# Split first loads, two banks for late outputs, and three moved operations in a six-stage decoder kernel

## The chip, the cores and the metric

The kernel runs on one core of one Trainium2 chip. The metric is device time in microseconds (us). The engines are TensorE (PE in the profile; its weight loads are PEld), VectorE (DVE), ScalarE (ACT), GpSimd (POOL) and SyncE (SP), whose queue issues most DMAs.

## The reference

Input `x` is 32 sequences ("items") of 100 rows by 256, and a context of 32 x 361 x 192. Six residual blocks follow one another, each on a plain layer norm of `x`:

```
x = x + self_attention(norm(x))              # 16 heads of 16, causal
x = x + cross_attention(ctx, norm(x), mask)  # 4 heads of 64, keys: ctx rows and latents
x = x + block(norm(x))                       # rope attention, then 8 experts, top 2
x = x + rotated_attention(norm(x))
x = x + wide_cross_attention(norm(x), ctx)   # 16 heads of 64
x = x + shared(norm(x)) + experts(norm(x))   # shared MLP 256-1024-256, and top 2 of 8 experts
```

In the last block every row is sent to two experts, and their outputs are weighted and added to the row, as is the output of the shared MLP.

## The kernel before

All 32 items stay in on-chip memory as `g.x`. There is one block of code for each stage: `self_phase`, `normed_cross_phase`, `mix_phase` (the "mixed" stage), `rotation_phase`, `wide_cross_phase` and `expert_phase`. Between two stages all engines meet. Within a stage the order of the work is written out by hand, for each engine apart, in pairs of items; semaphores tie the engines to one another, and each engine works strictly down its own list.

**Self stage.** SP issues the list `g.loads` in order, each load with the semaphore of its set. The set `first` holds 8 items, the qkv weights, the constants and the projection weights; `rest` holds the other 24 items. PE, ACT and DVE all begin with a wait for the whole of `first`. PE then runs `WARM` = 4 products on the qkv weights that nobody reads, and goes on to `make_rows` (L259, which transposes the normed pair), `make_q`, `make_k` (L266), `make_v` (L281), `mask` and `scores` (L296). DVE measures a pair (L85, L89), POOL takes the root (L94, L96), DVE applies it (L101), and ACT copies every bank out (L408 for the transposed rows).

**Cross stage.** SP loads the context rows (`load_cross_raw`) of a pair into one buffer, `raw`, as soon as the statistics of the pair before are taken (`cstats`). At the head DVE does `keep_kv` (L2093), measures the keys (L2103, L2107), and scales them with `norm_k` (L2112) once POOL has the root (L1688). `ctx_stats(SECOND)` (L2074 to L2085) stands between `norm_k(FIRST, 0, 1)` and `norm_k(FIRST, 1, 0)`. PE's `turn_k` (L1785) transposes the scaled keys.

**Mixed stage.** ACT's list begins with `apply(1)` (L1196, which norms the second pair and waits for POOL's offset at L768), then `keep_rows(0)` (L1133), then `keep_rope(0)` (L1137). PE transposes the normed first pair (L862), waits until it is copied, transposes the rope rows (L862 again) and makes q (L880).

**Expert stage, its end.** When the 57 tiles of the experts are done, POOL gathers the two expert rows of each item by two indirect DMAs (L3731), with a one-column add to `combine_hold` (L3729) ahead of them. DVE adds them to `g.x` (`combine`, L4074 and L4076) and copies the indices for the item 8 further on. Meanwhile PE does the shared MLP of the seven pairs 1, 3, ..., 13: hidden layer (L3539), turn of the next pair (L3549), output (`later_out`, L3834) into one bank, `out_bank`. `add_later` (L4087) adds that bank to `g.x`; `later_out(j)` waits for `add_later(j - 1)`, which stands behind `combine(4j + 1)` in DVE's list. SP stores the items in order (L3695), those of the seven pairs after their `add_later`.

## Time and profile before

| | |
|---|---|
| median of 3 runs | 3362.42 us (3358.3 to 3364.45) |
| profiled execution, device time | 3364.29 us |
| its span, first to last instruction | 3362.4 us |
| mean granted TensorE clock | 0.98 of full speed |
| PE busy | 3202.7 us (95%) |
| DVE, ACT, POOL busy | 53%, 48%, 44% |

All starts below are microseconds from the start of the span. A timeline row reads: start, length, engine, line, operation, output and inputs, how many instructions are merged; in brackets how long the engine stood idle before it, and who released it. The granted clock is a share of 2.4 GHz: 0.50 is 1.2 GHz.

### The profile page before, as it was taken

How to read it: one execution, taken by the hardware profiler on the slowest of the kernel's cores; microseconds unless marked ns; L12 is line 12 of the kernel's file. 1: busy time of each engine (PE TensorE's matmuls, PEld its weight loads, DVE VectorE, ACT ScalarE, POOL GpSimd, SP SyncE). 2: the span in 40 equal slices, each digit the busy share in tenths (PEclk: the TensorE clock that was granted, in tenths of full speed). 3: DMA queues.
4: the chain of work that ended last, by engine and by line, in shares of the span. 5: the costliest groups of instructions: out<-in, count | busy, mean ns of one | idle time of the engine just before them, and what ended most of it. 6: DMA issues, size and time to landing. Idle time of an engine off the chain costs nothing. (4 is left out here: it accounts for less than half of the span.)

```text
span 3362.4 us, 71194 instructions
## 1 busy us (share of the span) xinstructions
PE 3202.7 (95%) x26568; PEld 2352.6 (70%) x26569; DVE 1772.9 (53%) x5682; ACT 1607.3 (48%) x3295; POOL 1494.3 (44%) x1990
## 2 busy tenths in 40 slices
PE   7998999998999779998999999999999999999998
PEld 5775566666777644444676777767777688999997
DVE  4666777765888556543455544554445565111114
ACT  4654666665666047884555445545455511111111
POOL 1002444433676146651665656655666564000017
PEclk9999999998999889999999999999999999999999
DMA  8700111100001650000000000000000013999963
GB/s 244 290 2 14 43 43 44 43 15 14 17 23 29 172 143 24 21 16 26 14 8 8 8 8 15 8 8 8 8 14 1 2 40 118 325 327 323 325 237 104
DMA packets 111490, 263.34 MB, mean 78 GB/s; under 512 B 24003, under 2 KB 70240, under 8 KB 95840
## 3 DMA queue, kind: packets, MB, share of 16 engines
q1 hardware_dynamic: 90208, 224.70, 21.0%
q0 software_dynamic: 16384, 26.29, 2.8%
q10 hardware_dynamic: 4608, 8.39, 0.7%
q8 instruction: 194, 3.18, 0.4%
q14 instruction: 96, 0.79, 0.1%
HBM read 196.61 MB, written 62.65 MB: 77 GB/s over the span
## 5 line engine op out<-in xcount | busy, mean ns | idle before, releaser
L3004 POOL TENSOR_SCALAR wide_probs<-wide_probs,wide_inverse 100x361 f32<-100x361 f32 x504 | 594.5, 1192 | 0.1
L3297 ACT ACTIVATE wide_probs<-wide_probs,wide_least 100x361 f32<-100x361 f32 x512 | 301.0, 592 | 6.8 <-DVE wide_least L3410 6.8
L3410 DVE CUSTOM_DVE_ANT_0 wide_probs<-banks,wide_bias 100x361 f32<-100x361 f32 x512 | 251.5, 529 | 42.8 <-issue 37.7
L3056 PE MATMUL banks<-w_wide_v,wide_c 64*120 64x512 f32 (+1 forms) x1152 | 266.0, 591 | 0.0
L3050 PE MATMUL banks<-wide_c,w_wide_k 64*128 64x361 f32 x1536 | 257.1, 467 | 2.3 <-PEq L4101 2.3
L2588 ACT ACTIVATE rot_h<-banks,w_rot_b 128x800 f32<-128x800 f32 x256 | 223.3, 923 | 54.7 <-PE banks L2414 49.1
L3002 POOL TENSOR_TENSOR wide_hold_pool<-eps 100x1 f32<-100x1 f32 x252 | 48.6, 193 | 444.7 <-DVE wide_inverse L3416 444.7
L3891 ACT ACTIVATE tiles_hT<-banks 128x512 f32<-128x512 f32 x114 | 68.1, 597 | 349.1 <-PE banks L3807 349.1
L3807 PEld LDWEIGHTS banks<-tiles_xT,tiles_w 128*128 128x128 f32 x1824 | 214.7, 194 | 4.7 <-issue 1.8
L3807 PE MATMUL banks<-tiles_xT,tiles_w 128*128 128x128 f32 x1824 | 215.3, 277 | 1.2 <-DVE tiles_xT L4053 1.2
L3050 PEld LDWEIGHTS banks<-wide_c,w_wide_k 64*128 64x128 f32 x1536 | 150.5, 188 | 90.8 <-issue 4.6
L3083 PE MATMUL banks<-wide_kT,wide_qT 64*100 64x361 f32 x1024 | 207.4, 476 | 1.8 <-issue 0.7
L3820 PE MATMUL banks<-tiles_w,tiles_hT 128*128 128x256 f32 x912 | 206.4, 379 | 0.3 <-issue 0.3
L3729 POOL TENSOR_TENSOR combine_hold<-eps 100x1 f32<-100x1 f32 x32 | 7.9, 246 | 434.0 <-DMA slots<-tiles_out 433.2
L3056 PEld LDWEIGHTS banks<-w_wide_v,wide_c 64*120 64x120 f32 (+1 forms) x1152 | 120.7, 180 | 106.0 <-issue 93.9
L3820 PEld LDWEIGHTS banks<-tiles_w,tiles_hT 128*128 128x128 f32 x912 | 168.8, 190 | 21.0 <-issue 0.4
L3291 ACT COPY wide_v<-banks 120x512 f32<-120x512 f32 (+1 forms) x96 | 56.2, 585 | 222.5 <-PE banks L3056 222.5
L3101 PEld LDWEIGHTS banks<-ident,wide_probs 100*120 100x120 f32 (+1 forms) x1536 | 139.7, 138 | 30.1 <-issue 28.2
L3101 PE MATMUL banks<-ident,wide_probs 100*120 100x100 f32 (+1 forms) x1536 | 155.9, 251 | 0.8 <-ACT wide_probsT L3303 0.8
L3113 PE MATMUL banks<-wide_probsT,wide_v 120*64 120x100 f32 (+1 forms) x3072 | 147.8, 251 | 4.1 <-ACT wide_probsT L3303 4.0
L3288 ACT COPY wide_kT<-banks 128x361 f32<-128x361 f32 x128 | 59.0, 461 | 193.2 <-PE banks L3050 193.2
L3113 PEld LDWEIGHTS banks<-wide_probsT,wide_v 120*64 120x64 f32 (+1 forms) x3072 | 134.6, 136 | 20.6 <-issue 17.6
(499 smaller groups left out, 7173.2 us busy)
## 6 DMA issues: line engine op xcount, KB each, us to landing
tiles_w<-in_moe_w SPq DMA_DIRECT2D x114, 1024.0 KB, 5.2
slots<-zeros SPq DMA_DIRECT2D x58, 512.0 KB, 6.6
cross_c<-in_ctxT SPq DMA_DIRECT2D x32, 270.8 KB, 4.4
wide_c<-in_ctxT SPq DMA_DIRECT2D x32, 270.8 KB, 4.1
mix_kT<-slots SPq DMA_DIRECT2D x32, 256.0 KB, 4.3
slots<-mix_m_tiles_out ACTq DMA_DIRECT2D x32, 256.0 KB, 4.1
tiles_rows<-slots SPq DMA_DIRECT2D x57, 128.0 KB, 4.8
slots<-tiles_out SPq DMA_DIRECT2D x57, 128.0 KB, 5.0
```

The lines of the kernel that those rows point to most:

```text
L2588: nc.scalar.activation(t.h[:, u % 2, m, 2 * half:2 * half + 2, :], pair_banks(i), ACT.Tanh, bias=w.b1[:, m:m + 1]).then_inc(h_done[i], 1)
L3004: last = nc.gpsimd.tensor_scalar(t.probs[:, i, j, :], t.probs[:, i, j, :], t.inverse[:, i, j:j + 1], None, ALU.mult)
L3050: last = nc.tensor.matmul(make_bank(unit, lane)[:, 0:CTX], w.k[rows_of(lane), k, at:at + P], g.wide_c[rows_of(lane), of.buf, k, :], start= ...
L3056: last = nc.tensor.matmul(make_bank(unit, lane)[0:kw, :], g.wide_c[rows_of(lane), of.buf, k, k0:k0 + kw], w.v[rows_of(lane), k, of.hf * BA ...
L3083: last = nc.tensor.matmul(scores(j), t.qT[rows_of(j), here.hf, m, lane, :], t.kT[rows_of(j), here.hf, m, lane, :], start=True, stop=True)
L3101: last = nc.tensor.transpose(turned(bank)[0:cols, at], t.probs[:, i, j, k0:k0 + cols], g.ident[0:S, 0:S])
L3113: last = nc.tensor.matmul(out[rows_of(j), :], t.v[0:kw, of.hf, k, LANE_OF(i), at:at + WD], t.probsT[0:kw, group % STEP_GROUPS, bank, cols] ...
L3297: last = nc.scalar.activation(t.probs[:, i, j, :], t.probs[:, i, j, :], ACT.Exp, bias=t.least[:, i, j:j + 1], scale=-1.0, accum_out=t.rows ...
L3410: last = nc.vector.tensor_tensor_reduce(t.probs[:, i, j, :], scores(j), t.bias[:, :], -1.0, LARGEST, ALU.add, ALU.min, t.least[:, i, j:j + 1])
L3807: last = nc.tensor.matmul(out_, t.w1[:, lane, c, m * P:(m + 1) * P], t.xT[:, lane, c, :], start=(c == 0), stop=(c == DC - 1))
L3820: last = nc.tensor.matmul(tile_out, t.hT[:, lane, m, :], t.w2[:, lane, m, :], start=(m == 0), stop=(m == HM - 1))
L3891: nc.scalar.activation(t.hT[:, lane, half * HALF_HID:(half + 1) * HALF_HID, :].rearrange("p m r -> p (m r)"), hid_bank(lane, half), ACT.Si ...
```

## The change

- Self stage: the loads are cut into sets `pair` (2 items), `turn` (the identity), `qkv`, `first` (constants, items 2 to 7, projection weights), `near` (items 8 to 11 and two constants) and `rest`. Each step waits for the set that it reads. PE runs 3 unread products, on a buffer of zeros, before it waits for any load. ACT runs one exponential on a constant column, before its first wait on another engine's work.
- Cross stage: the context rows of the second pair are loaded by SP at the end of its self-stage list. `ctx_stats(SECOND)` and `ctx_root(SECOND)` stand ahead of the first pair's work.
- Mixed stage: ACT's `apply(1)` comes after `keep_rows(0)` and `keep_rope(0)`.
- Expert stage: `later_out` alternates between banks 6 and 7 and waits for the `add_later` two before; the add to `combine_hold` and its semaphore are gone; the last `add_later` stands after the last `combine`, and SP stores the last of the seven pairs at the end.

```diff
+NEAR_ITEMS = 12
+SELF_WARM = 3
...
             with sp.Fori(0, FILLS) as k:
...
+            sp.wait_ge(cs.cstats, 1)
+            for lane in range(LANES):
+                load_cross_raw(sp, near, lane, LANES + lane, ctx_in)
...
         def _(pe):
-            pe.wait_ge(g.loaded.first, g.total.first)
-            pe.wait_ge(s.ones, 1)
-            pe.wait_ge(s.parts_zero, 1)
-            for k in range(WARM):
-                nc.tensor.matmul(make_bank, w.qkv[:, 0, 0:P], w.qkv[:, 0, 0:BANK], start=True, stop=True)
+            pe.wait_ge(g.loaded.filled, 3)
+            for k in range(SELF_WARM):
+                nc.tensor.matmul(make_bank, g.zeros[:, 0:P], g.zeros[:, 0:BANK], start=True, stop=True)
+            pe.wait_ge(g.loaded.turn, g.total.turn)
...
             def make_q(p):
                 pe.wait_ge(s.yT, p + 1)
+                if p == 0:
+                    pe.wait_ge(g.loaded.qkv, g.total.qkv)
...
             def mask(b):
                 if b > 0:
                     pe.wait_ge(s.shifted, b)
+                else:
+                    pe.wait_ge(g.loaded.first, g.total.first)
...
         def _(act):
-            act.wait_ge(g.loaded.first, g.total.first)
-            act.wait_ge(s.picked, 1)
+            act.wait_ge(g.loaded.filled, 3)
+            nc.scalar.activation(t.begun[:, :], g.eps[:, :], ACT.Exp)
...
             def keep_k(p, edge):
+                if p == 0:
+                    act.wait_ge(s.picked, 1)
...
         def _(dve):
-            dve.wait_ge(g.loaded.first, g.total.first)
-            nc.vector.memset(parts_out, 0.0).then_inc(s.parts_zero, 1)
-            nc.vector.reduce_sum(t.own[:, :], g.own_scaled[:, :].rearrange("p (j i) -> p i j", i=EDGES), AX.X).then_inc(s.picked, 1)
-
             def stats(p):
-                if p == 2:
+                if p == 0:
+                    dve.wait_ge(g.loaded.pair, g.total.pair)
+                elif p == 1:
+                    dve.wait_ge(g.loaded.first, g.total.first)
+                elif p == 2:
+                    dve.wait_ge(g.loaded.near, g.total.near)
+                elif p * LANES == NEAR_ITEMS:
                     dve.wait_ge(g.loaded.rest, g.total.rest)
...
             stats(0)
+            nc.vector.memset(parts_out, 0.0).then_inc(s.parts_zero, 1)
             apply(0)
+            dve.wait_ge(g.loaded.first, g.total.first)
+            nc.vector.reduce_sum(t.own[:, :], g.own_scaled[:, :].rearrange("p (j i) -> p i j", i=EDGES), AX.X).then_inc(s.picked, 1)
...
+                if k + 1 == 0:
+                    apply(1)
                 if is_lane(n):
                     weigh(n)
...
-                if is_pair(k + MIX_AHEAD):
+                if k + MIX_AHEAD > 1 and is_pair(k + MIX_AHEAD):
                     apply(k + MIX_AHEAD)
...
-            for k in range(1, TURNS + 1):
+            for k in range(2, TURNS + 1):
...
             rows_root(SECOND)
+            ctx_root(SECOND)
             add_bias(FIRST)
...
             q_root(FIRST)
-            ctx_root(SECOND)
             add_bias(SECOND)
...
             rows_stats(SECOND)
+            ctx_stats(SECOND)
             dve.wait_ge(s.row, 1)
...
             norm_k(FIRST, 0, 1)
-            ctx_stats(SECOND)
             norm_k(FIRST, 1, 0)
...
+        later_bank = lambda j: g.psum[0:S, 6 + j % 2, :]
...
-            for b in range(B):
+            in_last_pair = lambda b: b // LANES == LATER_PAIRS[-1]
+            for b in sorted(range(B), key=in_last_pair):
                 sp.wait_ge(z.rows, b + 1)
...
                 pool.wait_ge(z.slots, b + 1)
-                nc.gpsimd.tensor_tensor(v.hold[:, k:k + 1], g.eps[0:S, :], g.eps[0:S, :], ALU.add).then_inc(z.held, 1)
...
             def later_out(j):
-                if j > 0:
-                    pe.wait_ge(z.shared, j)
+                if j > 1:
+                    pe.wait_ge(z.shared, j - 1)
...
                 if b + GATHER < B:
-                    dve.wait_ge(z.held, b + 1)
                     dve.wait_ge(z.rows, b + 1)
...
-                if step == 1 and j > 0:
+                if step == 1 and 0 < j < LATER:
                     add_later(j - 1)
+            add_later(LATER - 1)
...
+                load_items("pair", 0, LANES)
+                load_constant("turn", "ident")
+                self_w = Fields(qkv=weight(own, "qkv", "self_qkv", [P, DC, 3 * D]))
+                for n in ("own_scaled", "causal", "ident_b"):
+                    load_constant("first", n)
+                load_items("first", LANES, first_pairs)
                 self_w["proj"] = weight(own, "first", "self_proj", [P, DC, D])
+                load_items("near", first_pairs, NEAR_ITEMS)
+                for n in ("ones", "before"):
+                    load_constant("near", n)
+                load_items("rest", NEAR_ITEMS, B)
```

How the lists of the engines stand at three places follows. First VectorE at the head of the cross stage, from the second pair's row statistics on; before:

```order
L2063 TENSOR_SCALAR cross_rvareps<-cross_rmeanvar 100x2
L2093 SCALAR_TENSOR_TENSOR cross_kv<-banks,cross_crstd,cross_row 121x2x256 x2
...
L2112 TENSOR_TENSOR cross_kv<-cross_kv,cross_kroot 121x512
L2074 BN_STATS cross_cstats<-cross_raw 121x6 x6
L2077 MEMSET cross_hold 121x1
L2080 BN_AGGR cross_cmeanvar<-cross_cstats 121x2 x6
L2085 TENSOR_SCALAR cross_cvareps<-cross_cmeanvar 121x6
L2112 TENSOR_TENSOR cross_kv<-cross_kv,cross_kroot 121x512 x2
```

and in the changed kernel:

```order
L2083 TENSOR_SCALAR cross_rvareps<-cross_rmeanvar 100x2
L2094 BN_STATS cross_cstats<-cross_raw 121x6 x6
L2097 MEMSET cross_hold 121x1
L2100 BN_AGGR cross_cmeanvar<-cross_cstats 121x2 x6
L2105 TENSOR_SCALAR cross_cvareps<-cross_cmeanvar 121x6
L2113 SCALAR_TENSOR_TENSOR cross_kv<-banks,cross_crstd,cross_row 121x2x256 x2
...
L2132 TENSOR_TENSOR cross_kv<-cross_kv,cross_kroot 121x512 x3
```

The fourteen instructions of the context statistics stood between the second and the third key scaling; they now stand ahead of the first `keep_kv`, and the last three scalings follow each other.

Second ScalarE at the head of the mixed stage (`mix_y` is the normed pair, `mix_yT` and `mix_m_ropeT` the transposed rows); before:

```order
L1196 ACTIVATE mix_y<-x,mix_m_offset,mix_ln_rstd 100x256 x2
L1133 COPY mix_yT<-banks 128x400
L1137 COPY mix_m_ropeT<-banks 128x400
L1142 ACTIVATE mix_qT<-banks,w_mix_in_b 128x200
L1149 ACTIVATE mix_kT<-banks,mix_m_k_bias,mix_own 128x200 x2
```

and in the changed kernel:

```order
L1151 COPY mix_yT<-banks 128x400
L1155 COPY mix_m_ropeT<-banks 128x400
L1214 ACTIVATE mix_y<-x,mix_m_offset,mix_ln_rstd 100x256 x2
L1160 ACTIVATE mix_qT<-banks,w_mix_in_b 128x200
L1167 ACTIVATE mix_kT<-banks,mix_m_k_bias,mix_own 128x200 x2
```

Two copies have moved ahead of the two instructions that norm the second pair.

Third VectorE at the end of the program, the last items' `combine` (two rows each) and the last `add_later` (100x512); before:

```order
L4087 TENSOR_TENSOR x<-x,banks 100x512
L4074 SCALAR_TENSOR_TENSOR x<-combine_got,moe_gate,x 100x256
L4076 SCALAR_TENSOR_TENSOR x<-combine_got,moe_gate,x 100x256
L4074 SCALAR_TENSOR_TENSOR x<-combine_got,moe_gate,x 100x256
L4076 SCALAR_TENSOR_TENSOR x<-combine_got,moe_gate,x 100x256
```

and in the changed kernel:

```order
L4095 SCALAR_TENSOR_TENSOR x<-combine_got,moe_gate,x 100x256
L4097 SCALAR_TENSOR_TENSOR x<-combine_got,moe_gate,x 100x256
L4095 SCALAR_TENSOR_TENSOR x<-combine_got,moe_gate,x 100x256
L4097 SCALAR_TENSOR_TENSOR x<-combine_got,moe_gate,x 100x256
L4107 TENSOR_TENSOR x<-x,banks 100x512
```

The add of the last pair has moved behind the last two items.

## Rows read from the trace of the kernel before

**Rows 1.** The page, chain that ended last: share of the span by engine.
```profile
PE 18%; POOL 1%; DVE 0%; DMA 0%; issue 0%; SPq 0%; ACT 0%; DVEq 0%
```

**Rows 2.** Windows: stretch, length, busy PE, PEld, DVE, ACT, POOL, clock, DMA, GB/s.
```profile
50.00:150.00 100.00, 98.47 (x1109) 77.85 (x1108) 63.41 (x102) 60.76 (x92) 8.82 (x26) 1.00 0.93 342
```

**Rows 3.** Timeline of the first 22 us.
```profile
0.80 0.95 POOL L230 MEMSET zeros<- 128x1024 f32 x1
...
9.10 0.39 DVE L488 MEMSET banks<- 128x400 f32 x1 [8.98 <-DMA w_self_proj<-in_self_proj]
...
9.64 6.54 PE L250 MATMUL banks<-w_self_qkv 128*128 128x512 f32 x8 [9.64 <-DVE banks L488]
...
12.20 0.41 DVE L101 TENSOR_SCALAR self_y<-x,self_ln_meanvar,self_ln_rstd 100x256 f32<-100x256 f32 x1 [0.45 <-POOL self_ln_rstd L96]
...
16.02 0.51 PE L259 MATMUL banks<-ident,self_y 100*128 100x100 f32 x4
...
16.63 1.28 ACT L408 ACT_TABLE_LOAD   x1 [16.50 <-PE banks L259]
...
18.47 2.73 PE L266 MATMUL banks<-self_yT,w_self_qkv 128*128 128x200 f32 x8 [1.95 <-ACT self_yT L408]
```

**Rows 4.** Windows of the first loads; the last column is GB/s.
```profile
1.50:3.00 1.50, 0.00 (x0) 0.00 (x0) 0.00 (x0) 0.00 (x0) 0.52 (x2) 1.00 0.41 118
3.00:4.50 1.50, 0.00 (x0) 0.00 (x0) 0.00 (x0) 0.00 (x0) 0.00 (x0) 1.00 1.06 302
4.50:6.00 1.50, 0.00 (x0) 0.00 (x0) 0.00 (x0) 0.00 (x0) 0.00 (x0) 1.00 0.96 348
```

**Rows 5.** Timeline of the head of the cross stage.
```profile
306.80 1.41 DVE L2093 SCALAR_TENSOR_TENSOR cross_kv<-banks,cross_crstd,cross_row 121x512 f32<-121x512 f32 x2 [3.08 <-PE banks L1746]
...
319.76 3.23 POOL L1688 TENSOR_TENSOR cross_kroot<-cross_kclip,neg_half 121x8 f32<-121x8 f32 x2 [0.65 <-DVE cross_kclip L2107]
...
320.98 1.65 DVE L2074 BATCH_NORM_STATS2 cross_cstats<-cross_raw 121x6 f32<-121x192 f32 x6
...
323.37 1.28 DVE L2112 TENSOR_TENSOR cross_kv<-cross_kv,cross_kroot 121x512 f32<-121x512 f32 x2
...
324.20 3.33 PE L1785 MATMUL banks<-ident,cross_kv 124*128 124x124 f32 x16 [4.55 <-DVE cross_kv L2112]
```

**Rows 6.** Timeline of the head of the mixed stage.
```profile
769.97 0.51 PE L862 MATMUL banks<-ident,mix_y 100*128 100x100 f32 x4
...
771.31 0.78 POOL L785 TENSOR_TENSOR mix_m_rope<-mix_m_rope_a,mix_m_rope_b 100x256 f32<-100x256 f32 x1
...
774.44 1.09 ACT L1196 ACTIVATE mix_y<-x,mix_m_offset,mix_ln_rstd 100x256 f32<-100x256 f32 x2 [12.76 <-POOL mix_m_offset L768]
...
776.05 0.90 PE L862 MATMUL banks<-ident,mix_m_rope 100*128 100x100 f32 x4 [5.58 <-ACT mix_yT L1133]
```

**Rows 7.** Windows of two slow stretches, in the self and the cross stage.
```profile
19.00:29.00 10.00, 8.25 (x22) 6.29 (x21) 0.00 (x0) 1.57 (x3) 0.00 (x0) 0.50 0.93 190
...
322.00:332.00 10.00, 7.80 (x34) 5.86 (x36) 3.89 (x19) 1.85 (x2) 4.01 (x4) 0.53 0.21 57
```

**Rows 8.** Timeline of the end.
```profile
3264.88 1.02 POOL L3731 DMA_INDIRECT combine_got<-slots,combine_slot_i  x1 [0.30 <-issue]
...
3283.77 9.62 PE L3834 MATMUL banks<-w_moe_shared,combine_hidden 128*100 128x256 f32 x32 [4.67 <-DVE x L4087]
...
3298.98 7.07 PE L3834 MATMUL banks<-w_moe_shared,combine_hidden 128*100 128x256 f32 x32
...
3356.42 0.69 DVE L4087 TENSOR_TENSOR x<-x,banks 100x512 f32<-100x512 f32 x1 [4.25 <-PE banks L3834]
...
3358.45 0.48 DVE L4076 SCALAR_TENSOR_TENSOR x<-combine_got,moe_gate,x 100x256 f32<-100x256 f32 x1
```

**Rows 9.** The gathers' line: durations in ns, first and last start; time to landing.
```profile
L3731 POOL DMA_INDIRECT combine_got<-slots,combine_slot_i x64: 1007/1018/1290, 3263.5 to 3352.9; - x64
...
DMA to landing us min/median/max: 2.8/3.0/4.0
```

More of the change, by code:

```diff
@@ L175, in self_phase @@
         t = buffers(nc, ctx, "self", y=[S, TURNS, LANES, D], yT=[P, DC, LANES, S], qT=[P, TURNS, DC, LANES, S], kT=[P, TURNS, DC, EDGES, LANES, S], v=[S, TURNS, LANES, NH, HD + 1],
-                    rowmax=[S, 2, NH], probs=[S, 2, NH, S], probsT=[S, NH, S], parts=[P, ROUNDS, S], rowsum=[S, 2, NH], heads=[S, 2, D], headsT=[P, DC, S], own=[P, EDGES])
+                    rowmax=[S, 2, NH], probs=[S, 2, NH, S], probsT=[S, NH, S], parts=[P, ROUNDS, S], rowsum=[S, 2, NH], heads=[S, 2, D], headsT=[P, DC, S], own=[P, EDGES], begun=[P, 1])
         m1 = norm_of(nc, ctx, "self_ln")
@@ L3576, in expert_phase @@
         t = buffers(nc, ctx, "tiles", w1=[P, LANES, DC, HID], w2=[P, LANES, HM, D], rows=[P, LANES, D], xT=[P, LANES, DC, P], hT=[P, LANES, HM, P], out=[P, LANES, D])
[L3578 removed]
+        z = semaphores(nc, ctx, "combine", "slots half rows y yT_ready yT out_ready shared")
         later_hid_ready, later_hid = ([ctx.enter_context(nc.semaphore(f"combine_{n}{half}")) for half in range(2)] for n in ("hid_ready", "hid"))
         gathered, stored = ([ctx.enter_context(nc.semaphore(f"combine_{n}{k}")) for k in range(GATHER)] for n in ("gathered", "stored"))
[L3581 removed]
+        v = buffers(nc, ctx, "combine", got=[S, GATHER, 2, D], y=[S, LANES, D], yT=[P, DC, LANES, S], hidden=[P, HM, LANES, S])
         gather_i = ctx.enter_context(nc.sbuf_tensor("combine_slot_i", [S, GATHER, 2], I32))
@@ L3833, in later_out @@
                             pe.wait_ge(later_hid[m // HALF_HID], j + 1)
-                        last = nc.tensor.matmul(out_bank[:, lane * D:(lane + 1) * D], v.hidden[:, m, lane, :], w.shared2[:, m, :], start=(m == 0), stop=(m == HM - 1))
+                        last = nc.tensor.matmul(later_bank(j)[:, lane * D:(lane + 1) * D], v.hidden[:, m, lane, :], w.shared2[:, m, :], start=(m == 0), stop=(m == HM - 1))
                 last.then_inc(z.out_ready, 1)
@@ L4086, in add_later @@
                 rows = g.x[:, b:b + LANES, :].rearrange("s l d -> s (l d)")
-                nc.vector.tensor_tensor(rows, rows, out_bank, ALU.add).then_inc(z.shared, 1)
+                nc.vector.tensor_tensor(rows, rows, later_bank(j), ALU.add).then_inc(z.shared, 1)
             apply_later(1)
@@ L4113, in decoder @@
         g.psum = ctx.enter_context(nc.psum_tensor("banks", [P, 8, BANK], F32))
-        sets = "first rest cross mix mix_b rot wide moe cleared"
+        sets = "pair turn qkv near first rest cross mix mix_b rot wide moe cleared"
         g.loaded = Fields(**{n: ctx.enter_context(nc.semaphore("loaded_" + n)) for n in sets.split() + ["filled"]})
@@ L4168, in decoder, with load_items, load_constant @@
             with ExitStack() as own:
-                load("first", g.x[:, 0:first_pairs, :], i["x"][0:first_pairs].rearrange("b s d -> s b d"))
-                self_w = Fields(qkv=weight(own, "first", "self_qkv", [P, DC, 3 * D]))
-                for n in ("ident", "own_scaled", "causal", "ident_b", "ones", "before"):
-                    t = g[n]
-                    load("first", t[tuple(slice(None) for _ in t.shape)], i[n].bitcast(t.dtype))
+                def load_items(which, start, end):
+                    load(which, g.x[:, start:end, :], i["x"][start:end].rearrange("b s d -> s b d"))
+                def load_constant(which, n):
+                    load(which, g[n][tuple(slice(None) for _ in g[n].shape)], i[n].bitcast(g[n].dtype))
+                load_items("pair", 0, LANES)
[4 more added lines that the diff above has]
+                load_items("first", LANES, first_pairs)
                 self_w["proj"] = weight(own, "first", "self_proj", [P, DC, D])
-                load("rest", g.x[:, first_pairs:B, :], i["x"][first_pairs:B].rearrange("b s d -> s b d"))
+                load_items("near", first_pairs, NEAR_ITEMS)
+                for n in ("ones", "before"):
+                    load_constant("near", n)
+                load_items("rest", NEAR_ITEMS, B)
                 g.loads += cross_loads + mix_loads + rot_loads + moe_loads
```

5 lines of the change are left out of this document (3 added, 2 removed).

## The prediction

> **What bounds the kernel now.** I read the chain that ended last first [rows 1]: PE has by far the largest share, and what is not on it is small. Then the windows of the self loop [rows 2]: PE busy 98.47 of 100 us. So in the loops an earlier start passes through unchanged, and a gain can only come from stretches in which PE stands idle or runs at the lower of its two clocks. The timeline shows four of these, and the four parts of the change sit on them: PE's first useful work at 16.02 [rows 3]; 4.55 us idle at the head of the cross stage [rows 5]; 5.58 us idle at the head of the mixed stage [rows 6]; 4.67 us idle in the last hundred microseconds, followed by output products that take 9.62 instead of 7.07 us [rows 8]. I take the four as independent: each stage begins when all engines have met, and what follows waits for data of its own stage.
>
> **First loads.** Before, every engine waited for the last load of `first`; VectorE went on at 9.10, the normed pair was ready at 12.20 + 0.41 = 12.61, but PE was inside its unread products until 9.64 + 6.54 = 16.18, so the transposes ran at 16.02, and then ScalarE loaded its function table for 1.28 us before it could copy; q began at 18.47 [rows 3]. After: the pair is 205 KB. The queue had moved 1.5 x 118 = 177 KB by 3.0 us and goes on at 302 GB/s [rows 4], so the pair is in at about 3.1. The identity (66 KB) and qkv (786 KB) make 1057 KB, in at 4.5 + (1057 - 630)/348 = 5.7. VectorE needed 3.5 us from its wait to both normed items, 0.39 of it for the memset, which now lies in its wait for the root: 3.2 + 3.1 = 6.3. PE: the zeros are filled at 1.75; six product records at the length of before, 6.54/8 = 0.82 to 0.85 us each, from 1.9 to 7.0. So the transposes start at 7.0, not at 6.3: the unread products are what is late next. Without the table load the rest takes 0.51 + 0.1 + 0.49 + 0.05: q at 8.2 instead of 18.47, **-10.3 us**. The other loads are not met: `first` lands near 9 as before and is needed by the mask and the second copy of k, ten microseconds later; `near` is 443 KB more, near 10.5, and wanted after the first scores. If the pair lands 2 us late, transposes start at 8.3 and the term is -9.0.
>
> The clock belongs to this term. From 19 to 29 it was granted at 0.50, with PE busy 8.25 of 10 us [rows 7]; q took 2.73 us [rows 3]. In the self loop at 1.00 the same eight records take 1.6 us, by the ratio of the two levels (2.73/2 = 1.4, plus the weight loads) an estimate. q, k, v and their like at full clock are worth about 4.1 us. Before, the clock fell in the 1.95 us in which PE waited for the table and the copy. In the new order this gap is about 0.6 us, so if the unread products bring the clock up, it stays up. Whether 5.1 us of them are enough no row tells: nothing excludes either. I take half, **-2.0**, and keep 0 and -4.1 as ends.
> The Trainium skill ("TensorE: Matmul & The Clock Gate", What's actually happening) says that PE's recent activity sets the clock and that the point of the rise varies from run to run; the trace agrees as far as it shows a fall behind a gap, and by that page both ends are possible for one and the same kernel.
> The Trainium skill ("ScalarE: Activation LUTs", What ACT_TABLE_LOAD costs) gives 1.28 us for the load and a further 1.38 us of drain for a switch. This trace shows 1.28, and the copy 0.02 us behind it, so there is no drain here; with it the sum would be 1.4 us larger.
>
> **Cross stage.** The context statistics of the second pair took VectorE from 320.98 to 323.37 + 0.1, in front of the last two key scalings. Their roots came from POOL at about 321.4 and 323.0 (two operations, 3.23 us from 319.76), so the first scaling can start at 321.4 instead of 323.37 and PE's transposes at 322.25 instead of 324.20; the second scaling ends at 323.7, before PE has done the first half (half of 3.33 us): **-1.9 us** [rows 5]. In the new place the 2.45 us start at 303.7, where VectorE's wait of 3.08 us for the first keys began, and end at 306.2; that wait ended at 306.80 [rows 5]; margin 0.6. Without that cover (rows not loaded in time) it would cost up to 2.45. They are loaded some 35 us ahead, behind SP's last zero fill, and nothing but SP waits there. POOL's root for them, 1.3 us, moves to 306.2, where POOL had nothing urgent. The stretch after this gap ran at 0.53 [rows 7]; a gap that is 1.9 us shorter may keep the clock up, worth up to 2.5 us more. I take 0 for that and keep 2.5.
>
> **Mixed stage.** PE had transposed the first pair by 770.5, and the rope rows were ready at 771.31 + 0.78 = 772.1, but ScalarE stood in `apply(1)` until 774.44 + 1.09 and copied only then [rows 6]. Now it copies at 770.6 to 771.1; PE's second transposes start at 772.2 instead of 776.05: **-3.85 us**. `apply(1)` then begins at 774.44 as before, when its offset is there, and ends at 775.5; it is wanted by nothing before the second pair, and the copy of q, at 772.2 + 4.6 = 776.8, comes after it. If it did collide it would cost 1.1 us. Lower end -2.7, upper end -3.85 - 4, if the clock stays up there too.
>
> **The end.** (a) With two banks the second output follows its hidden layer: 4.67 us of idle and 9.62 - 7.07 = 2.55 us of low clock go, 7.2 us on PE's chain. The later turns, copies and adds are early enough: VectorE's adds come 5 us or more before PE wants a bank back. PE would end at 3356.4 - 7.2 = 3349.2 [rows 8]. (b) But then the gathers are late next. The last one starts at 3352.9 and lands 3.0 us later [rows 9]; they are 64, issued by POOL. Two in direct succession start 1.35 us apart (3264.88, behind the first at 3263.5 [rows 8, 9]). Without the add between items, 63 x 1.35 = 85.1 us from 3263.2: the last starts at 3348.3 and lands at 3351.3. Its item takes VectorE 1.0 us and the add 0.69: 3353.1. (c) Before, VectorE ended at 3358.45 + 0.48 = 3358.93, one store later the span, at 3362.4: 3.5 us. Now two stores follow: + 0.4, end at 3357.0, **-5.4 us**. Bounds: if POOL's pace does not change, last landing 3355.5 and end 3361.2, -1.2; if PE alone bounds, 3349.2 + 0.7 + 3.9 = 3353.8, -8.6.
>
> **Sum.** 10.3 + 2.0 + 1.9 + 3.85 + 5.4 = 23.4 us. Against the profiled execution's own 3364.29 us that is 3340.9; the median shown is 1.9 us lower, 3339.0. I forecast **3340 us**.
>
> **Rivals.**
> 1. *Clock up at the heads*: 4.1 instead of 2.0 in the self stage, 2.5 more in the cross stage, 2 in the mixed: gain 30, 3332 to 3334. For it: each of the falls stands behind a gap of 2 us or more that becomes shorter. Against: at each head PE still waits several times for ScalarE's copies.
> 2. *Gains that don't land*: the clock stays low, POOL's pace is as before (the gap before a gather is 0.30 us of issue where the add had 0.18, so little may go), and the pair lands late: 9.0 + 1.9 + 2.7 + 1.2 = 14.8, 3348 to 3350.
> 3. *No gain*: an early start given back in the self stage, because the 98.47 us in 100 hides a fixed end: loads or zero fills that must be done. Against it: DMA is at 0.93 until 150 us [rows 2] and the stage ends at 300. It would leave 11, 3352, or with the other losses within 0.2% of before.
> 4. *Slower*: the clock does not rise in the self loop. PE's work in 100 us of it would take about 190 at half clock. The other parts give 11 us or so, and the earlier start 10; the loss passes that after about 24 us in the loop at low clock, and 50 us of it gives 3385. Against it: from 29 on the clock was at 1.00 as soon as the products came without gaps, and the loop is the same.
>
> **How the numbers follow.** The forecast's case 0.5 (3336 to 3346), rival 1 0.22, rival 2 0.18, rival 3 0.05, rival 4 0.03, other 0.02. A difference under 0.2% (6.7 us) can't be told from no change here. Faster by more than that: all but part of rival 3, and rival 4: 0.93; within 0.2%: 0.04; slower 0.03. Range: from rival 1's best, 3331, to rival 2's worst, 3350, which leaves out rivals 3 and 4 and the far ends.
>
> **What would show it.** Right: q's first product near 8.2 (near 7.7 with the clock up), transposes behind the unread products and not behind the load; the cross stage's key transposes 2 us earlier from its head; ScalarE's first copy in the mixed stage 3.9 us earlier from its head; no wait of the second output; the last add behind the last item, gathers 1.35 us apart. Wrong: transposes that wait for the pair's load; a PE wait in the self loop that was not there; gathers still 2.8 us per item, with VectorE waiting for them at the end; a copy of q that waits behind `apply(1)`.

## The result, and the profile after

The changed kernel takes 3334.78 us (median of 4 runs, 3334.01 to 3336.59); the kernel before, timed beside it, 3361.22 us (4 runs, 3358.30 to 3364.45). The ratio is 0.9922, 95% interval 0.991 to 0.9934: 26.4 us less. The forecast was 3340 us, a gain of 23.4; the time lies inside the range. The profiled execution took 3334.01 us, 30.3 less than that of before (3364.29), and it is the pair of profiled executions that the traces compare.

The marks of the stages, read from the two timelines (start of the first instruction named, us):

| mark | before | after | difference | added in the part |
|---|---|---|---|---|
| cross stage, POOL's first memset | 301.85 | 288.22 | -13.63 | self: -13.6 |
| mixed stage, POOL's first memset | 766.16 | 746.81 | -19.35 | cross: -5.7 |
| first exponential of the mixed stage | 792.03 | 766.17 | -25.86 | mixed head: -6.5 |
| routing, first memset | 2697.99 | 2674.74 | -23.25 | 2.6 given back |
| first gather of the end | 3263.53 | 3240.54 | -22.99 | 0.3 given back |
| end of the span | 3362.4 | 3332.2 | -30.2 | end: -7.2 |

Timeline of the changed kernel's first microseconds, against [rows 3]:
```profile
0.71 1.28 ACT L415 ACT_TABLE_LOAD   x1 [0.58 <-PEq L4314]
1.81 5.10 PE L253 MATMUL banks<-zeros 128*128 128x512 f32 x6 [1.81 <-POOL zeros L235]
...
3.91 0.75 DVE L85 BATCH_NORM_STATS2 self_ln_stats<-x 100x6 f32<-100x256 f32 x2 [3.79 <-DMA x<-in_x]
...
7.27 0.54 PE L263 MATMUL banks<-ident,self_y 100*128 100x100 f32 x4 [0.36 <-DVE self_y L101]
...
8.86 1.59 PE L270 MATMUL banks<-self_yT,w_self_qkv 128*128 128x200 f32 x8 [1.05 <-DMA w_self_qkv<-in_self_qkv]
11.03 1.62 PE L270 MATMUL banks<-self_yT,w_self_qkv 128*128 128x200 f32 x8 [0.58 <-ACT self_qT L423]
13.88 1.97 PE L287 MATMUL banks<-w_self_qkv,self_yT 128*100 128x256 f32 x8 [1.23 <-ACT self_kT L429]
```
q starts at 8.86 instead of 18.47. Its releaser is a load, not ScalarE's copy: the first weight came about half a microsecond late. The transposes waited 0.36 us for VectorE and not for the unread products: VectorE was late because the pair had landed at 3.79, so here the forecast's order of the two was the wrong way round, by that 0.36 us. And q takes 1.59 us where before it took 2.73.

Windows of the first loads, against [rows 4]:
```profile
3.00:4.50 1.50, 1.50 (x3) 0.50 (x2) 0.59 (x2) 0.00 (x0) 0.00 (x0) 1.00 0.94 338
4.50:6.00 1.50, 1.50 (x3) 0.68 (x2) 0.96 (x6) 0.00 (x0) 0.92 (x3) 1.00 0.85 268
6.00:9.00 3.00, 1.59 (x7) 0.55 (x6) 0.67 (x2) 0.49 (x1) 0.62 (x1) 1.00 0.79 227
```
The last column is GB/s: where the forecast went on with 348, the rate fell to 268 and 227.

Windows of the self head and of the head of the cross stage, against [rows 7]:
```profile
9.00:19.00 10.00, 7.61 (x51) 5.71 (x52) 3.81 (x9) 2.65 (x5) 2.20 (x5) 1.00 0.70 169
19.00:29.00 10.00, 7.93 (x90) 6.30 (x89) 7.31 (x11) 6.46 (x8) 1.44 (x4) 1.00 0.93 198
302.00:312.00 10.00, 6.65 (x40) 6.01 (x42) 5.21 (x11) 4.92 (x8) 5.79 (x5) 0.83 0.00 0
```
The clock is at 1.00 from 19 to 29, where it was 0.50. In the cross stage 3.4 us at half clock are left of about 10.

Timeline of the head of the cross stage after, against [rows 5]:
```profile
288.40 2.84 PE L1766 MATMUL banks<-w_cross_kv,cross_c 64*121 64x512 f32 x12 [1.86 <-PEq L4122]
...
291.72 0.17 DVE L2105 TENSOR_SCALAR cross_cvareps<-cross_cmeanvar 121x6 f32<-121x6 f32 x1
291.93 0.75 DVE L2113 SCALAR_TENSOR_TENSOR cross_kv<-banks,cross_crstd,cross_row 121x512 f32<-121x512 f32 x1
...
306.09 0.69 DVE L2132 TENSOR_TENSOR cross_kv<-cross_kv,cross_kroot 121x512 f32<-121x512 f32 x1 [0.36 <-POOL cross_kroot L1708]
306.93 3.38 PE L1805 MATMUL banks<-ident,cross_kv 124*128 124x124 f32 x16 [2.62 <-DVE cross_kv L2132]
307.69 0.69 DVE L2132 TENSOR_TENSOR cross_kv<-cross_kv,cross_kroot 121x512 f32<-121x512 f32 x1 [0.91 <-POOL cross_kroot L1708]
```
Both scalings now wait for POOL's roots, as forecast. The key transposes stand 18.71 us behind the stage's start, where they stood at 22.35. Of these 3.64 us, 1.94 are the removed statistics and 1.70 are the first products, 2.84 instead of 4.54 us: those are the clock. The moved statistics end at 291.89, 0.65 us after the first products (288.40 + 2.84): with products at full clock the margin of 0.6 that the forecast gave them was used up, and they held the first key copy back by about half a microsecond. PE's path did not feel it: the second products and the next key copy are 1.70 us earlier from the stage's start, like the end of the first products.

Timeline of the head of the mixed stage after, against [rows 6]:
```profile
751.24 0.49 ACT L1151 COPY mix_yT<-banks 128x400 f32<-128x400 f32 x1 [8.88 <-PE banks L880]
...
752.80 0.56 PE L880 MATMUL banks<-ident,mix_m_rope 100*128 100x100 f32 x4 [1.67 <-POOL mix_m_rope L803]
...
753.94 3.04 PE L898 MATMUL banks<-mix_m_ropeT,w_mix_qkv 128*128 128x200 f32 x8 [0.58 <-ACT mix_m_ropeT L1155]
755.02 1.09 ACT L1214 ACTIVATE mix_y<-x,mix_m_offset,mix_ln_rstd 100x256 f32<-100x256 f32 x2 [1.12 <-POOL mix_m_offset L786]
...
757.59 1.59 PE L898 MATMUL banks<-mix_m_ropeT,w_mix_qkv 128*128 128x200 f32 x8 [0.61 <-DVE mix_qT L1507]
```
ScalarE copies first and norms the second pair while PE makes q. q still runs at half clock (3.04), k does not (1.59).

Timeline of the end after, and the line of the gathers, against [rows 8, 9]:
```profile
3319.11 7.07 PE L3855 MATMUL banks<-w_moe_shared,combine_hidden 128*100 128x256 f32 x32
...
3324.25 1.01 POOL L3752 DMA_INDIRECT combine_got<-slots,combine_slot_i  x1 [0.30 <-issue]
...
3327.46 0.48 DVE L4095 SCALAR_TENSOR_TENSOR x<-combine_got,moe_gate,x 100x256 f32<-100x256 f32 x1 [1.86 <-DMA combine_got<-slots,combine_slot_i]
...
3328.38 0.68 DVE L4107 TENSOR_TENSOR x<-x,banks 100x512 f32<-100x512 f32 x1
```
```profile
L3752 POOL DMA_INDIRECT combine_got<-slots,combine_slot_i x64: 1007/1011/1267, 3240.5 to 3324.3; - x64
```
PE is done at 3326.2, VectorE adds the last pair at 3328.4 behind a gather that it waited for: the gathers bound the end, 83.7 us from first to last.

### The profile page after: what moved, and what is told of

Its sections match the earlier page's. It is cut to its first block and busy times, and to the rows that moved or that the text cites. A ratio compares the mean times of both kernels' runs of the same rounds, so it can differ in the third digit from the quotient of the medians.

```text
span 3332.2 us, 71139 instructions
## 1 busy us (share of the span) xinstructions
PE 3190.6 (96%) x26566; PEld 2348.0 (70%) x26567; DVE 1772.6 (53%) x5682; ACT 1607.8 (48%) x3296; POOL 1486.0 (45%) x1958
## 5 line engine op out<-in xcount | busy, mean ns | idle before, releaser
L3752 POOL DMA_INDIRECT combine_got<-slots,combine_slot_i x64 | 65.5, 1024 | 452.7 <-DMA slots<-tiles_out 433.5
L3121 PEld LDWEIGHTS banks<-ident,wide_probs 100*120 100x120 f32 (+1 forms) x1536 | 139.4, 138 | 30.3 <-issue 28.2
L3446 DVE COPY wide_probsT<-banks 121x400 f32<-121x400 f32 x128 | 72.9, 570 | 144.0 <-PE banks L3121 144.0
```

The costliest lines, as they stand in the source:

```text
L3121: last = nc.tensor.transpose(turned(bank)[0:cols, at], t.probs[:, i, j, k0:k0 + cols], g.ident[0:S, 0:S])
L3752: nc.gpsimd.indirect_dma_start(v.got[:, k, j, :], None, slots[:, :], bass.IndirectOffsetOnAxis(ap=gather_i[:, k, j:j + 1], axis=0)).then_i ...
```

## The experiments

The first four were made to tell start from clock, part by part; each is compared with the kernel before, timed beside it.

**self_alone** is the kernel before with all edits of the self stage: the split loads, the products on `g.zeros`, `t.begun`, and the waits moved to where the data are needed.

> The kernel before with the self stage's part of the change alone (split loads, unread products on the zeros, table loaded early). Theory (start plus clock): the cross stage starts 13.6 us earlier than before, as in the changed kernel: q near 8.9 and the granted clock 1.00 from 19 to 29. Time 3361.2 - 13.6 = 3347.6. Rival (start alone, the clock is another part's doing): 9.6 to 10.3 us earlier, 3351, and 0.50 from where q begins.

Measured: 3351.52 us, ratio 0.9974 (0.9962 to 0.9985), 9.8 us less. In its profiled execution the cross stage starts at 288.01 and q at 8.62, and q, k and v take 1.59, 1.62 and 1.97 us. So the trace says 13.8 less where the medians say 9.8 (5.0 to 12.8). The likely reason lies in the kernel before, and it showed in the next three runs, which leave its self stage as it was:

| kernel | q starts | q, k, v take | cross stage starts |
|---|---|---|---|
| before | 18.47 | 2.73, 3.03, 3.48 | 301.85 |
| cross_alone | 18.35 | 1.62, 1.62, 1.97 | 297.73 |
| mixed_alone | 17.17 | 1.62, 1.62, 1.97 | 296.56 |
| end_alone | 16.90 | 1.62, 1.62, 1.97 | 296.29 |

The same instructions, with the same gap of 1.95 us ahead of q, ran at full clock in three executions and at half clock in one, the one that I had taken as the profile of before. Timeline of cross_alone, which stands for the three:
```profile
10.17 5.88 PE L253 MATMUL banks<-w_self_qkv 128*128 128x512 f32 x8 [10.17 <-DVE banks L491]
15.89 0.51 PE L262 MATMUL banks<-ident,self_y 100*128 100x100 f32 x4
18.35 1.62 PE L269 MATMUL banks<-self_yT,w_self_qkv 128*128 128x200 f32 x8 [1.95 <-ACT self_yT L411]
20.55 1.62 PE L269 MATMUL banks<-self_yT,w_self_qkv 128*128 128x200 f32 x8 [0.58 <-ACT self_qT L415]
```
The 44 executions of before timed in the two usual jobs spread from 3356.25 to 3364.95 us. The five executions with the old start (these and early_table, below) also took 5.12, 5.31, 5.88, 6.54 and 6.65 us for the same eight records of unread products. The Trainium skill ("TensorE: Matmul & The Clock Gate", What's actually happening) says that the point of the rise differs from run to run of one kernel; these durations agree. The fall behind them, in one of the five, is worth 4.1 us.

**cross_alone** is the kernel before with the cross stage's edits and no other. Its diff, without the two lines that move POOL's `ctx_root(SECOND)` and the one that starts SP's later loads at the third pair:
```diff
+            sp.wait_ge(cs.cstats, 1)
+            for lane in range(LANES):
+                load_cross_raw(sp, near, lane, LANES + lane, ctx_in)
...
             rows_stats(SECOND)
+            ctx_stats(SECOND)
...
             norm_k(FIRST, 0, 1)
-            ctx_stats(SECOND)
```


> The kernel before with the cross stage's part alone (context rows of two pairs loaded early, context statistics moved ahead of the key products). Theory (order): the key transposes start 1.9 us earlier, counted from the stage's start; what the changed kernel gained beyond that there (5.7 us from the stage's start to the next stage) hung on the clock in which the stage happened to begin, so this kernel gains 1.9 to 2.5 us: 3359. Rival (the shorter gap keeps the clock up by itself): 4 to 5.7 us, 3356, with the clock at 1.00 behind the gap.

Measured: 3361.20 us, ratio 0.9999 (0.999 to 1.0008): no difference, spread 3355.71 to 3367.82 over 11 runs. The key transposes did come 1.95 us earlier from the stage's start (20.40 against 22.35, with first products of 4.52 and 4.54 us), so the order does what it was said to do; self_alone and the changed kernel, both with first products of 2.84 us, give the same 1.95 (20.66 and 18.71). But behind them the clock was low for 10.2 us as before, and the stage was 464.6 us long against 464.3: the 2 us were lost again to stretches at half clock, one of them at 740 to 746, which the execution of before did not have. Neither the theory's 2 us nor the rival's 4 to 5.7 shows in the median; its interval reaches to 3.4 us less, so it shuts out the rival and not the theory. Windows of cross_alone and then of self_alone, around the transposes:
```profile
314.00:330.00 16.00, 13.31 (x57) 8.56 (x58) 7.66 (x24) 6.10 (x12) 7.91 (x7) 0.68 0.01 1
```
```profile
302.00:318.00 16.00, 11.30 (x52) 8.41 (x54) 9.74 (x36) 5.82 (x11) 9.11 (x7) 0.68 0.13 36
```
16 us at 0.68 are 10.2 at half clock in both, with the shorter gap (2.63) and with the longer (4.57). Other executions had none of it behind the same 2.62 us: one_bank and no_products, below, whose code here is that of the changed kernel. Window of one_bank:
```profile
302.00:318.00 16.00, 12.39 (x74) 7.49 (x75) 10.78 (x32) 7.39 (x15) 8.15 (x7) 1.00 0.00 1
```
And end_alone had about 3.5 us at half clock behind the longer gap (4.56). So the length of the gap does not settle the clock here; what does stays open.

**mixed_alone** is the kernel before with ScalarE's order changed:
```diff
+                if k + 1 == 0:
+                    apply(1)
                 if is_lane(n):
                     weigh(n)
...
-                if is_pair(k + MIX_AHEAD):
+                if k + MIX_AHEAD > 1 and is_pair(k + MIX_AHEAD):
                     apply(k + MIX_AHEAD)
```


> The kernel before with the mixed stage's part alone (ScalarE copies the first rows ahead of the second norm). Theory (order plus clock): second transposes 3.9 us earlier from the stage's start and the first exponential 6.4 us earlier, since k, mask and scores run at full clock: 3361.2 - 6.4 = 3354.8. Rival (order alone): 3.9 us, 3357.3, with the clock at 0.50 up to the scores as before.

Measured: 3353.62 us, ratio 0.9978 (0.9969 to 0.9987), 7.7 us less. The first exponential stands 19.37 us behind the stage's start, against 25.87 in before: 6.5 us, the theory. ScalarE's row after (one copy, then the other, then the norm):
```profile
764.69 0.49 ACT L1133 COPY mix_yT<-banks 128x400 f32<-128x400 f32 x1 [8.76 <-PE banks L862]
767.00 0.49 ACT L1137 COPY mix_m_ropeT<-banks 128x400 f32<-128x400 f32 x1 [1.82 <-PE banks L862]
768.62 1.09 ACT L1196 ACTIVATE mix_y<-x,mix_m_offset,mix_ln_rstd 100x256 f32<-100x256 f32 x2 [1.13 <-POOL mix_m_offset L768]
```
The stretch is steadier than the others: 25.7 to 25.9 us in four of the five profiles with the old order (23.6 in the fifth), 19.3 to 19.4 in six of the eight with the new order and no added product there (20.5 and 21.6 in the other two).

**end_alone** is the kernel before with two banks, without the add, and with the last pair stored last:
```diff
-                nc.gpsimd.tensor_tensor(v.hold[:, k:k + 1], g.eps[0:S, :], g.eps[0:S, :], ALU.add).then_inc(z.held, 1)
...
-                if j > 0:
-                    pe.wait_ge(z.shared, j)
+                if j > 1:
+                    pe.wait_ge(z.shared, j - 1)
```


> The kernel before with the end's part alone (two banks for the shared outputs, no add between gathers, last pair stored last). Theory (gathers' pace bounds once the bank's wait is gone): from the first gather to the end 7.2 us less, last gather 83.8 us behind the first and not 89.4: 3354.0. Rival (my forecast's step, 5.4 us): 3355.8. Rival (it needs the earlier stages' shift): 0 to 2 us.

Measured: 3355.69 us, ratio 0.9981 (0.9972 to 0.999), 5.6 us less. In the trace the last gather starts 83.6 us behind the first and the span ends 91.4 us behind it (98.9 in before): the theory's 7.2 us are there, 7.5. The median cannot tell 7.5 from 5.4.

**no_products** is the changed kernel without these two lines:
```diff
-            for k in range(SELF_WARM):
-                nc.tensor.matmul(make_bank, g.zeros[:, 0:P], g.zeros[:, 0:BANK], start=True, stop=True)
```


> The changed kernel without the three unread products ahead of the first transposes; PE's first work is then the transposes at 7.3 us. Theory (the products bring the clock up, the load of qkv hides them): q still begins at 8.6 to 8.9, but q, k and v take 2.73, 3.03 and 3.48 us as in the profiled execution before, not 1.59, 1.62 and 1.97; 4.1 us slower than the changed kernel, 3339. Rival (the clock is up without them, since the granted clock reads 1.00 from the first microsecond): the same durations, the same time, 3334.8.

**after_again** is the changed kernel, not edited, in the same job.

> The changed kernel once more, unchanged, for more executions of it. Theory (clock at the heads of the stages differs between executions of one kernel, at the cross head most): median 3334.8 again with a spread of 4 us or more, and another length of low clock behind the cross stage's key transposes than 3.4 us. Rival (the new order fixes the clock there): spread under 3 us as in the first four runs, and the same stretch.

Measured: in this job every kernel took longer, before itself 3393.34 us, so only ratios and stretches within it count. after_again took 3372.76 us (ratio 0.9939, 0.9924 to 0.9955: 20.6 us less than before); no_products 3377.80, 5.0 us more than after_again. Timeline of no_products, and its window:
```profile
7.14 0.90 PE L261 MATMUL banks<-ident,self_y 100*128 100x100 f32 x4 [7.14 <-DVE self_y L101]
8.80 3.00 PE L268 MATMUL banks<-self_yT,w_self_qkv 128*128 128x200 f32 x8 [0.76 <-DMA w_self_qkv<-in_self_qkv]
12.38 3.04 PE L268 MATMUL banks<-self_yT,w_self_qkv 128*128 128x200 f32 x8 [0.58 <-ACT self_qT L421]
16.65 3.73 PE L285 MATMUL banks<-w_self_qkv,self_yT 128*100 128x256 f32 x8 [1.23 <-ACT self_kT L427]
```
```profile
9.00:20.00 11.00, 9.18 (x24) 7.12 (x25) 2.27 (x8) 1.57 (x3) 2.21 (x5) 1.00 0.70 177
```
q starts when it did, k starts at 12.38 instead of 10.60 and the cross stage at 293.01 instead of 287.79, 5.2 us later. In the trace the theory holds, with 1 us more than it said: the products bring the clock up, at no cost, since q has to wait anyway. The two ratios alone (0.9958 and 0.9939) have intervals that overlap. In after_again the cross stage's transposes had 10.2 us at half clock behind them, not 3.4, so that stretch is not fixed by the order either; its times spread over 7.6 us (3371.24 to 3378.84). In the rotation and at the end after_again lost time of another kind, told at the end of this document.

**one_bank** and **hold_back** are the changed kernel with one half of the end's part undone each:
```diff
-        later_bank = lambda j: g.psum[0:S, 6 + j % 2, :]
+        later_bank = lambda j: g.psum[0:S, 6, :]
...
-                if j > 1:
-                    pe.wait_ge(z.shared, j - 1)
+                if j > 0:
+                    pe.wait_ge(z.shared, j)
```
```diff
+                nc.gpsimd.tensor_tensor(v.hold[:, k:k + 1], g.eps[0:S, :], g.eps[0:S, :], ALU.add).then_inc(z.held, 1)
                 for j in range(2):
```


> The changed kernel with one bank for the shared outputs, as before; the gathers keep their new pace. Theory (two chains end within 3 us of each other): PE waits 4.67 us for VectorE's first add and its output products take 9.62 us once, so PE ends 7.2 us later, 3333.4, and with the last add (0.7) and 3.1 us behind it the span is 3337.2: 5.0 us slower than the changed kernel, 3339.8. Rival (the gathers bound the end alone): 0 to 1 us.

> The changed kernel with the add between the gathers and its semaphore as before; two banks stay. Theory (POOL's pace bounds the end): last gather 89.4 us behind the first and not 83.8: 5.6 us slower than the changed kernel, 3340.4. Rival (before, the gathers were slow only because VectorE's adds, which free the buffers, stood behind PE): the gathers keep 83.8 to 85 and the time is 0 to 1 us more.

Both ran in the slower job (3372.51 and 3372.33 us, as after_again), and the engines' long stand at the end covers what was asked: inconclusive. They were run again in a job in which before took 3361.28 us.

> The changed kernel with one bank again, a second time: in the run one_bank PE, ScalarE and VectorE stood up to 20 us without a releaser among the shared outputs, which covers what was asked. Theory (two chains end within 3 us of each other): from the first gather to the span's end 96.7 us and not 91.7, since PE ends 7.2 us later: 5.0 us slower than the changed kernel. Rival (the gathers bound the end alone): 91.7 to 92.7.

> The changed kernel with the add between the gathers again, a second time, for the same reason. Theory (POOL's pace bounds the end): from the first gather to the last 89.4 us and to the span's end 97.3: 5.6 us slower than the changed kernel. Rival (before, the gathers were slow because VectorE stood behind PE): 84 to 85 us, to the span's end 92 to 93, 0 to 1 us slower.

Measured: one_bank_2 3337.54 us (ratio 0.9929, 0.9915 to 0.9942), hold_back_2 3341.16 (0.9942, 0.9928 to 0.9955). Timelines, of one_bank_2 and then of hold_back_2:
```profile
3265.99 9.94 PE L3855 MATMUL banks<-w_moe_shared,combine_hidden 128*100 128x256 f32 x32 [3.66 <-DVE x L4107]
...
3331.86 7.07 PE L3855 MATMUL banks<-w_moe_shared,combine_hidden 128*100 128x256 f32 x32
3338.96 0.69 DVE L4107 TENSOR_TENSOR x<-x,banks 100x512 f32<-100x512 f32 x1 [3.67 <-PE banks L3855]
```
```profile
3317.17 7.07 PE L3856 MATMUL banks<-w_moe_shared,combine_hidden 128*100 128x256 f32 x32
...
3327.86 1.01 POOL L3753 DMA_INDIRECT combine_got<-slots,combine_slot_i  x1 [0.30 <-issue]
...
3331.90 0.68 DVE L4109 TENSOR_TENSOR x<-x,banks 100x512 f32<-100x512 f32 x1
```
With one bank VectorE's last add waits 3.67 us for PE, and the span ends 95.9 us behind the first gather (3342.5 - 3246.59). With the add it waits for the last gather, 89.1 us behind the first, 10.7 us after PE began its last outputs, and the span ends at 96.9 (3335.7 - 3238.76). With neither it ends at 91.7, with both, in before, at 98.9. So undoing one half costs 4.2 or 5.2 us, and one half alone brings 3.0 or 2.0 of the 7.2: two chains of almost one length ended there, and both had to become shorter. In the traces the theory of each holds. The times only lean that way: hold_back_2 lies 6.4 us over the changed kernel, where 5.6 were expected, and one_bank_2 2.8 over it, where 5.0 were; the intervals of both overlap that of the changed kernel (0.991 to 0.9934).

**early_table** is the kernel before with one edit:
```diff
+            act.wait_ge(g.loaded.filled, 3)
+            nc.scalar.activation(t.begun[:, :], g.eps[:, :], ACT.Exp)
             act.wait_ge(g.loaded.first, g.total.first)
```


> The kernel before with one edit: ScalarE loads its function table while the first loads run. PE's gap ahead of q is then 0.6 and not 1.95 us. Theory (the clock falls in that gap, in about half of the executions of before): q begins 1.4 us earlier, and the slower half is gone: against before's median 1.4 + 2 = 3.5 us faster, no execution more than 2 us above the median. Rival (the gap does not decide, the products' start does): 1.4 us faster, and times spread over 6 us or more as before.

Measured: 3357.31 us, ratio 0.999 (0.9981 to 0.9999), 4.0 us less. Timeline:
```profile
10.42 6.65 PE L250 MATMUL banks<-w_self_qkv 128*128 128x512 f32 x8 [10.42 <-DVE banks L490]
16.91 0.51 PE L259 MATMUL banks<-ident,self_y 100*128 100x100 f32 x4
18.08 1.62 PE L266 MATMUL banks<-self_yT,w_self_qkv 128*128 128x200 f32 x8 [0.67 <-ACT self_yT L410]
```
q follows the start of the transposes by 1.17 us and not 2.45: the table load's 1.28 us exactly. Unread products as slow as in the profile of before (6.65 us, 6.54 there) were here followed by q at full clock. That leans towards the gap as a condition of the fall, but it is one execution, and three of four with the long gap had q at full clock too; the 4.0 us fit 1.3 plus the clock in half of the executions. But the runs still spread over 6.7 us (3355.29 to 3361.95), three of eleven more than 2 us above the median, as the rival had it, and the interval reaches down to 0.3 us: the theory is not shown by this.

**kept_and_q_first** tries to beat the changed kernel:
```diff
             pe.wait_ge(s.qT, FIRST.n)
+            nc.tensor.matmul(keys_bank(0, 0), w.lkv[:, 0, 0:P], w.lkv[:, 0, 0:BANK], start=True, stop=True)
             pe.wait_ge(s.filled, 4)
...
+                pe.wait_ge(s.yT, p + 1)
+                if p == 0:
+                    nc.tensor.matmul(make_bank[:, 0:FILL_COLS], w.qkv[:, 0, 0:P], w.qkv[:, 0, 0:FILL_COLS], start=True, stop=True)
                 pe.wait_ge(z.rope, (p + 1) * LANES)
-                pe.wait_ge(s.yT, p + 1)
...
+                load("q0", self_w.qkv[:, :, 0:D], i["self_qkv"][:, :, 0:D])
+                load("qkv", self_w.qkv[:, :, D:3 * D], i["self_qkv"][:, :, D:3 * D])
```


> The changed kernel with three edits meant to beat it: one unread product (512 columns) in PE's gap ahead of the first key transposes of the cross stage, one (288 columns) ahead of the second transposes of the mixed stage, and q's columns of the first weight loaded by themselves ahead of the rest. Theory (PE kept busy in the gap keeps the clock up): no low clock behind the key transposes of the cross stage (3.4 us of it at half in the changed kernel, 1.7 us of work) and q, k of the mixed stage 1.6 us each, not 3.04 for q; q of the self stage begins 0.0 to 0.5 us earlier: 3 us faster in all, 3331.5. Rival (the clock falls or not whatever the gap, or the products come late and delay the transposes): 0 to 1 us either way.

Measured: 3333.73 us (3330.48 to 3338.52), ratio 0.9924 (0.991 to 0.9937). Its profiled execution has the shortest span of all, 3328.6 us, but the time is not told apart from the changed kernel's. Its windows and timeline:
```profile
302.00:312.00 10.00, 7.48 (x48) 5.31 (x50) 4.97 (x12) 4.83 (x8) 6.57 (x5) 1.00 0.01 2
```
```profile
304.67 1.10 PE L1949 MATMUL banks<-w_cross_lkv 128*128 128x512 f32 x2 [0.82 <-ACT cross_qT L1981]
306.47 1.00 PE L1810 MATMUL banks<-ident,cross_kv 124*128 124x124 f32 x8 [0.70 <-DVE cross_kv L2138]
308.07 1.00 PE L1810 MATMUL banks<-ident,cross_kv 124*128 124x124 f32 x8 [0.60 <-DVE cross_kv L2138]
...
754.06 1.62 PE L903 MATMUL banks<-mix_m_ropeT,w_mix_qkv 128*128 128x200 f32 x8 [0.58 <-ACT mix_m_ropeT L1160]
```
In the mixed stage the mechanism works: q takes 1.62 us, against 2.7 to 3.0 in the thirteen other profiles. In the cross stage it is not shown: there is no low clock behind the key transposes, but one_bank and no_products had none either, without the product. Both places pay less than the 3 us because the work behind was not waiting for PE alone. The transposes at full clock wait 0.60 us for the second scaling, and the products of the scores follow the start of the transposes 0.8 us sooner, not 1.7; the stage as a whole took 459.2 us, no less than the changed kernel's 458.6. In the mixed stage the first exponential stands at 18.22 us and not 19.36, 1.1 us less. q of the self stage started at 8.32, behind the copy.

## Why the prediction was right, and where it was short

- **The forecast** of faster, 3340 us within 3331 to 3350, held. All four parts worked at their places, and no stage took the gain back as rivals 3 and 4 would have it.
- **Self stage**, forecast -12.3 (start -10.3, clock -2.0). Between the profiled executions it was -13.6: the start -9.6 and the clock the whole 4.1, so here rival 1 came true. In no_products the same head without the unread products ran at half clock, and in all eight profiles with them q took 1.59 to 1.62 us, so they are what brought the clock up. The pair landed at 3.8 and not 3.1, and the first weight near 8.8 and not 5.7: from 4.5 us on the loads ran at 268 and 227 GB/s and not at the 348 of [rows 4]. Against the kernel's median the part is worth 9.8 us; that the profile of before was one with the slow head, 4.1 us of it, explains the gap between the two figures but is not timed by itself. I had asked whether the clock would rise after; that it differs between executions of the kernel before I did not ask.
- **Cross stage**, forecast -1.9 with the clock's share at nothing. The step is right to 0.05 us (1.94 in the changed kernel, 1.95 alone). The further 3.8 us came of the clock in which the stage's head happened to run, and after_again lacked 2.6 of them (461.2 us for the stage, not 458.6). Over all profiles the stage takes 462.3 to 466.8 us with the old order (5 profiles), and with the new one, without an added product, 457.8 to 461.2 in six and 464.6 and 465.9 in two. What the part is worth in the median stays open between nothing (cross_alone) and the 3.9 us by which the two means differ, an estimate from 13 profiles of two kinds of job.
- **Mixed stage**, forecast -3.85. The wait is right (3.90 from the stage's start to the second transposes). The term was short by 2.6 us, the clock: k at 1.59 and not 3.00, mask and scores likewise. I had kept this as an upper end and taken nothing, though [rows 6] show a gap of 5.58 us that by the forecast's own times (770.5 to 772.2) was to become 1.7; this step of the sum failed in its size, and mixed_alone shows it by itself.
- **End**, forecast -5.4, measured -7.2. The chain was right: two banks move PE's end, and the gathers are late next. The pitch was 1.33 us (83.7/63) and not 1.35, which makes 1.3 us, and 3.1 us passed from the last add to the end of the span, not 3.9; the first gather stood 0.3 later than the forecast's 3263.2.
- **The sum** was 23.4 and the median's gain 26.4. The four parts alone bring 9.8 + 0.1 + 7.7 + 5.6 = 23.2, each with an interval of 3 to 4 us to either side, so whether they help each other can't be said. A sum made of one execution of before, 30.3 when compared with one of after, holds 4 us of the draw of the clock: read from the two profiles alone, rival 1 with its gain of 30 looks like the one that came true. That 23.4 lies so near the median's 26.4 is in part luck. With the self stage at the usual head the profiles give 9.5 + 5.7 + 6.5 + 7.2 - 2.9 = 26.0: the self term was too large by 2.8, the cross, mixed and end terms too small by 3.8, 2.6 and 1.8, and 2.9 that no term had went the other way.
- **Given back**: 2.9 us between the first exponential of the mixed stage and the first gather, 1.7 of them ahead of the rotation stage's first gather; PE's longest wait for `mix_kT` from `slots` there was 11.4 instead of 11.1 us. The change need not be what took them: in the ten profiles of the usual jobs the way from that exponential to the routing's first memset took 1905.3 to 1906.5 us in six and 1908.4 to 1909.0 in four. Before and the changed kernel with one bank (one_bank_2) are among the six; the changed kernel, but also self_alone and early_table, whose code is there that of before, among the four. What sets it stays open.

## What to carry to other kernels

Read the head of a stage for its clock in more than one execution before you price it: a stretch that is at half clock in one profile may be at full clock in most. Where PE has to wait for a load anyway, products on data that are there can bring the clock up for the first real ones; here they cost nothing. At the end of a kernel compare the lengths of all chains that end there: two that end within 3 us of each other must both be shortened, and either alone shows as less than half of the gain.

## What the runs showed of the hardware that was not expected

- The granted clock in the windows is not to be trusted in the first 20 us of this program. no_products has 1.00 from 9 to 20 us while q, k and v take 3.00, 3.04 and 3.73 us, as long as they do at 0.50 in before. The durations tell the clock there: the changed kernel's first six product records of 128x512 took 5.10 us, 0.85 each, where eight of the cross stage (3.68 us at L1780) take 0.46 each.
- In the slower job (before took 3393.34 us in it) the engines other than POOL stood still for up to some 20 us among the shared outputs, each without a releaser of its own, while POOL started a gather every 1.31 us. PE and ScalarE of after_again, each from a timeline of its own:
```profile
3294.54 7.81 PE L3855 MATMUL banks<-w_moe_shared,combine_hidden 128*100 128x256 f32 x24 [18.80 <-issue]
```
```profile
3293.65 0.84 ACT L3930 ACTIVATE combine_hidden<-banks 128x800 f32<-128x800 f32 x1 [21.60 <-remote]
```
  All four profiles of that job have it (PE's longest wait for issue there 18.8, 14.7, 9.0 and 7.8 us), none of the usual jobs. From 3272 to 3296 after_again's instruction queues, which bring the engines their code, moved no packet, those of the changed kernel one each in the like stretch: that the engines waited for their code behind the gathers fits, but no run tests it. The same job took 361 us where the changed kernel took 355 for the rotation stage. Both stay open.
